# Softmax probabilities of two attention layers: halves formed in rows and transposed by DMA, in place of transposes on TensorE

## The reference, cut to what matters

```python
# layer 0
scores = jnp.einsum('bhid,bhjd->bhij', q, k) / np.sqrt(dh)
attn = jax.nn.softmax(scores, axis=-1)
out = jnp.zeros_like(q)
for r in range(Wv.shape[0]):
    v_r = (src @ Wv[r] + bv[r]).reshape(Bb, Nn, h, dh).transpose(0, 2, 1, 3)
    mask = (adj_matrix == r)[:, None]
    out = out + jnp.einsum('bhij,bhjd->bhid', attn * mask, v_r)
# ... projection, layer norm, feed forward with 1024 hidden, layer norm
# layer 1
e = jnp.einsum('whqd,whkd->whqk', q, k)
e = jnp.where(e >= 0, e, ALPHA * e)
attn = jax.nn.softmax(jnp.where(adj[:, None] > 0, e, NEG), axis=-1)
h = jnp.einsum('whqk,whkd->whqd', attn, v)
# ... layer norm, one product with the features beside it, layer norm
```

## Time and profile before

| | |
|---|---|
| median of 3 runs | 2848.8 us (2847.48 to 2848.91) |
| the profiled execution, its own time | 2849.84 us |
| its span in the trace | 2847.9 us |
| PE busy | 2697.4 us, 95% of the span |
| PE weight loads busy | 2224.1 us, 78% |
| DVE busy | 2246.5 us, 79% |
| ACT busy | 2246.4 us, 79% |
| POOL busy | 1628.7 us, 57% |
| mean granted TensorE clock | 0.988 |

### The profile page before, as it was taken

One profiled execution on the slowest core, in us unless ns is written; L12 is line 12 of the kernel. 1 busy time (PEld: TensorE's weight loads), 2 busy tenths in 40 slices (PEclk: granted clock), 3 DMA queues, 4 the chain that ended last, 5 costly groups with the idle time before them and its releaser, 6 DMA issues.

```text
span 2847.9 us, 86473 instructions
## 1 busy us (share of the span) xinstructions
PE 2697.4 (95%) x33544; PEld 2224.1 (78%) x33544; DVE 2246.5 (79%) x3986; ACT 2246.4 (79%) x6226; POOL 1628.7 (57%) x1870
## 2 busy tenths in 40 slices
PE   3899999999999999999999999999999999999985
PEld 2688888888878878878778788878788788888874
DVE  4588788888888887888888878878878878878863
ACT  3578878878878878878878878878878878878864
POOL 1355655655565565565565565565565565565563
PEclk9899999999999999999999999999999999999997
DMA  3000000000000000000000000000000000000000
GB/s 113 9 17 17 24 21 18 22 24 17 20 24 20 17 24 20 17 24 21 16 24 21 17 24 21 17 24 21 17 24 20 17 24 20 17 24 20 17 15 12
DMA packets 77909, 62.70 MB, mean 22 GB/s; under 512 B 6592, under 2 KB 76736, under 8 KB 77504
## 3 DMA queue, kind: packets, MB, share of 16 engines
q1 hardware_dynamic: 74336, 53.76, 6.2%
q10 hardware_dynamic: 3168, 3.41, 0.4%
HBM read 40.38 MB, written 16.78 MB: 20 GB/s over the span
## 4 chain that ended last, share of the span: by engine, by line
PE 55%; issue 24%; POOL 14%; DVE 4%; ACT 1%; POOLq 0%; DMA 0%; ACTq 0%
PE bank L420 40%; POOL edge_rows L1102 7%; PE bank L512 4%; PE bank L496 4%; POOL x1b L1150 3%; PE bank L484 3%; POOL oT L1169 3%; PE bank L437 3%; PE bank L465 2%; DVE o L1025 1%; DVE o_st L972 1%; DVE o_mv L976 1%; POOL o_ve L1124 0%; ACT p L705 0%; POOL o_rs L1126 0%
## 5 line engine op out<-in xcount | busy, mean ns | idle before, releaser
L935 DVE TENSOR_TENSOR pm<-pT,bank 128x4096 f16<-128x4096 f16 x256 | 568.4, 2282 | 25.8 <-issue 25.8
L420 PE MATMUL bank<-wv,xT 128*128 128x512 f16 (+1 forms) x2304 | 468.5, 344 | 0.0
L1169 POOL TENSOR_TENSOR oT<-oT_f,oT 128x512 f16<-128x512 f32 x64 | 74.4, 1163 | 606.6 <-ACT oT L805 606.6
L420 PE MATMUL bank<-yT,w 128*128 128x256 f16 x3072 | 367.1, 273 | 2.6 <-ACT oT_f L797 2.2
L705 ACT ACTIVATE p<-bank,p_nmax 128x128 f32<-128x128 f32 x1024 | 368.5, 423 | 0.0
L420 PEld LDWEIGHTS bank<-wv,xT 128*128 128x128 f16 x2304 | 226.1, 98 | 176.0 <-issue 0.3
L420 PE MATMUL bank<-w,h 128*128 128x256 f16 x3072 | 345.6, 272 | 1.7 <-POOL h L1154 1.7
L883 DVE TENSOR_TENSOR pT<-bank,pT 128x512 f16<-128x512 f32 x512 | 321.0, 675 | 10.8 <-ACT pT L779 5.8
L420 PEld LDWEIGHTS bank<-yT,w 128*128 128x128 f16 x3072 | 294.6, 98 | 40.4 <-ACT oT_f L797 2.7
L420 PEld LDWEIGHTS bank<-w,h 128*128 128x128 f16 x3072 | 295.9, 98 | 38.3 <-issue 1.9
L693 ACT ACTIVATE p<-p,p_nmax 128x128 f32<-128x128 f32 x1024 | 312.1, 390 | 0.8
(11 more groups left out here) (128 smaller groups left out, 5911.6 us busy)
## 6 DMA issues: line engine op xcount, KB each, us to landing
x_sb<-in_x_dram SPq DMA_DIRECT2D x64, 256.0 KB, 2.8
adj_i<-in_adj_dram SPq DMA_DIRECT2D x128, 128.0 KB, 2.7
out_dram<-out_sb SPq DMA_DIRECT2D x64, 256.0 KB, 2.1
pm<-in_L_gnn_W_dram ACTq DMA_DIRECT2D x1, 1024.0 KB, 14.0
pm<-in_L_gnn_W_dram SPq DMA_DIRECT2D x1, 1024.0 KB, 17.5
h_f<-in_L_gnn_Wffn_dram SPq DMA_DIRECT2D x1, 512.0 KB, 10.3
pm<-in_L_gnn_Wv_dram ACTq DMA_DIRECT2D x2, 256.0 KB, 10.6
pm<-in_L_gnn_Wv_dram SPq DMA_DIRECT2D x2, 256.0 KB, 11.0
```

What stands on the lines that cost most here:

```text
L420: last = nc.tensor.matmul(o, l, r, start=(first and k == 0), stop=(k == len(todo) - 1))
L935: V_.tensor_tensor(pm0[g][:, s], pT0[g][:, s].unsqueeze(1).broadcast_to([P, REL, HEADS, P]), edges[:, g].unsqueeze(2).broadcast_to([P, REL ...
L1169: V_.tensor_tensor(oT1[:, 1], oT1_f[:], oT1[:, 0], ALU.subtract).then_inc(S["oT1_lo"], 1)
```

## The change

In both layers the probabilities are split while they are still rows, and the halves are transposed by DMA from SBUF to SBUF:

- `transpose_probs` is gone from TensorE, and with it the eight jobs `pT0_*` and `pT1_*` of the bank table.
- Layer 0: `exp_0` writes its result back into the bank of the scores instead of `p0`; ACT copies the hi half from there into the new f16 tile `p0h` (`probs_high_0`), DVE writes the lo half (`probs_low_0`), each in four instructions by `r`. The banks of `s0_0` to `s0_3` are now freed by `p0_lo`, not by `p0_exp`.
- Layer 1: `exp_1` stays in SBUF; ACT copies the hi half into `p1h`, and POOL writes the lo half (`probs_low_1`, four instructions), which DVE did before.
- SP issues four transposing DMAs a step (`transpose_probs_0` and `transpose_probs_1`, one for each batch and layer), each of 16 blocks of 128x128 f16 with both halves of a batch: 512 KB. Before the first of a layer SP waits for all four lo halves of the pair. `by_edge_type` now waits for `pT0_in_g`, and `attend_1` for `pT1_in_g`.
- The pipeline is one pair deeper (5 instead of 4 extra steps): feed forward and the start of layer 1 now run for n-3, the attention of layer 1 for n-4, the last product for n-5. The order of jobs in all five lists is new, and so is the table of banks.
- `out_sb` is gone; the last addition is done in `x2b`, which is stored from there. Some jobs got a wait more (`values_0` for `xT0_lo`, `x_high` for q0 and k0, `x2_high` for q1 and k1).

The core of the diff (the table and the lists are cut to a few lines, since the order below shows them):

```diff
--- before.py
+++ after.py
...
 PE_BANKS = [
-    ("pT0_0", 3, 1, "pT0_lo", 4, 1),
...
+    ("v1", 1, 4, "v1_lo", 1, 1),
...
+    ("s0_0", 1, 0, "p0_lo", 4, 1),
...
-    ("s0_0", 3, 0, "p0_exp", 4, 1),
...
-        p0 = sb("p0", [ROWS, G, C, P])
+        p0h = sb("p0h", [G, 2, C, ROWS, P], F16)
+        p1h = sb("p1h", [G, 2, C, ROWS, P], F16)
...
-        pT1 = sb("pT1", [2, G, HEADS, P], F16)
+        pT1 = sb("pT1", [G, 2, HEADS, P], F16)
...
-        out_sb = sb("out_sb", [G, D])
...
+                def transpose_probs_0(m, g):
+                    sp.wait_ge(S["p0_lo"], 4 * m + 4)
+                    if past(m):
+                        sp.wait_ge(S["p0_masked"], 4 * m + 2 * g - 2)
+                    sp.dma_start_transpose(pT0[g][:].rearrange("p s h j -> p (s h) j"),
+                                           p0h[:, g].rearrange("p s c r j -> p (s c r j)")).then_inc(S[f"pT0_in_{g}"], 16)
+
+                def transpose_probs_1(m, g):
+                    sp.wait_ge(S["p1_lo"], 4 * m + 4)
+                    if past(m):
+                        sp.wait_ge(S["o1_ps"], 2 * m + g - 1)
+                    sp.dma_start_transpose(pT1[:, g].rearrange("p s h j -> p (s h) j"),
+                                           p1h[:, g].rearrange("p s c r j -> p (s c r j)")).then_inc(S[f"pT1_in_{g}"], 16)
+
                 def store(m):
                     sp.wait_ge(S["out_ready"], m + 1)
-                    sp.dma_start(out[bass.ds(m * G, G)].rearrange("g t d -> t g d"), out_sb[:]).then_inc(S["out_stored"], 16)
+                    sp.dma_start(out[bass.ds(m * G, G)].rearrange("g t d -> t g d"), x2b[:]).then_inc(S["out_stored"], 16)
 
                 def steps(n):
+                    if live(n - 1):
+                        transpose_probs_0(n - 1, 0)
                     if live(n):
                         load_x(n)
-                    if live(n - 1):
-                        load_adj0(n - 1)
+                        load_adj0(n)
+                    if live(n - 1):
+                        transpose_probs_0(n - 1, 1)
+                    if live(n - 4):
+                        transpose_probs_1(n - 4, 0)
+                        transpose_probs_1(n - 4, 1)
                     if live(n - 5):
                         store(n - 5)
-                    if live(n - 1):
-                        load_adj1(n - 1)
+                    if live(n - 2):
+                        load_adj1(n - 2)
 
                 pipeline(steps, 0, 5)
                 sp.wait_ge(S["out_stored"], 16 * PAIRS)
...
                 def values_0(m, i):
                     g, cols = i // 2, slice(i % 2 * BANK, (i % 2 + 1) * BANK)
                     bank_free(f"v0_{i}", m)
+                    pe.wait_ge(S["xT0_lo"], m + 1)
...
-                def transpose_probs(layer, p, m, g):
-                    pe.wait_ge(S[f"p{layer}_exp"], 4 * m + 4)
-                    for c in range(C):
-                        i = g * C + c
-                        bank_free(f"pT{layer}_{i}", m)
-                        for r in range(ROWS):
-                            last = nc.tensor.transpose(ps(f"pT{layer}_{i}")[:, r * P:(r + 1) * P], p[:, r, g, c], ident[:])
-                        last.then_inc(S[f"pT{layer}_ps"], 1)
-
...
-                        pe.wait_ge(S["pT1_lo"], 4 * m + 2 * g + 2)
+                        pe.wait_ge(S[f"pT1_in_{g}"], 16 * m + 16)
...
                 def steps(n):
-                    if live(n - 1):
-                        transpose_probs(0, p0, n - 1, 0)
+                    if live(n - 3):
+                        feed_forward(n - 3)
+                    if live(n - 4):
+                        values_1(n - 4)
+                    if live(n - 2):
+                        output_projection(n - 2)
...
-                        transpose_attention_1(n - 4)
+                        attend_0(n - 1, 0)
+                    if live(n - 3):
+                        scores(1, q1, k1, n - 3)
+                    if live(n - 4):
+                        attend_1(n - 4)
...
-                        act.wait_ge(S["pT1_ps"], 4 * m)
+                        act.wait_ge(S["p1_lo"], 4 * m + r - 3)
...
-                        act.wait_ge(S["pT0_ps"], 4 * m)
...
-                            last = nc.scalar.activation(p0[:, r, g, c], ps(f"s0_{r}")[:, at:at + P], ACT.Exp,
+                            last = nc.scalar.activation(ps(f"s0_{r}")[:, at:at + P], ps(f"s0_{r}")[:, at:at + P], ACT.Exp,
                                                         bias=p0_nmax[:, r, g, c:c + 1], accum_out=p0_sum[:, g, c, r:r + 1])
...
-                def probs_high_1(m, g):
-                    for c in range(C):
-                        i = g * C + c
-                        act.wait_ge(S["pT1_ps"], 4 * m + i + 1)
-                        if past(m):
-                            act.wait_ge(S["o1_ps"], 2 * m + g - 1)
-                        nc.scalar.activation(flat(pT1[:, 0, g, head_cols(c)]), ps(f"pT1_{i}")[:], copy).then_inc(S["pT1_hi"], 1)
+                def probs_high_1(m, r):
+                    act.wait_ge(S["p1_exp"], 4 * m + r + 1)
+                    if past(m):
+                        act.wait_ge(S["pT1_in_0"], 16 * m)
+                        act.wait_ge(S["pT1_in_1"], 16 * m)
+                    nc.scalar.activation(p1h[:, :, 0, :, r], p1[:, r], copy).then_inc(S["p1_hi"], 1)
...
-                def probs_high_0(m, g):
-                    for c in range(C):
-                        i = g * C + c
-                        act.wait_ge(S["pT0_ps"], 4 * m + i + 1)
-                        if past(m):
-                            act.wait_ge(S["p0_masked"], 4 * m + 2 * g - 2)
-                        nc.scalar.activation(flat(pT0[g][:, 0, head_cols(c)]), ps(f"pT0_{i}")[:], copy).then_inc(S["pT0_hi"], 1)
+                def probs_high_0(m, r):
+                    act.wait_ge(S["p0_exp"], 4 * m + r + 1)
+                    if past(m):
+                        act.wait_ge(S["pT0_in_0"], 16 * m)
+                        act.wait_ge(S["pT0_in_1"], 16 * m)
+                    nc.scalar.activation(p0h[:, :, 0, :, r], ps(f"s0_{r}")[:].rearrange("p (g c j) -> p g c j", g=G, c=C),
+                                         copy).then_inc(S["p0_hi"], 1)
...
-                def probs_low_0(m, g):
-                    for c in range(C):
-                        i = g * C + c
-                        dve.wait_ge(S["pT0_hi"], 4 * m + i + 1)
-                        low(flat(pT0[g][:, 1, head_cols(c)]), ps(f"pT0_{i}")[:], flat(pT0[g][:, 0, head_cols(c)])).then_inc(S["pT0_lo"], 1)
-
-                def probs_low_1(m, g):
-                    for c in range(C):
-                        i = g * C + c
-                        dve.wait_ge(S["pT1_hi"], 4 * m + i + 1)
-                        low(flat(pT1[:, 1, g, head_cols(c)]), ps(f"pT1_{i}")[:], flat(pT1[:, 0, g, head_cols(c)])).then_inc(S["pT1_lo"], 1)
+                def probs_low_0(m, r):
+                    dve.wait_ge(S["p0_hi"], 4 * m + r + 1)
+                    low(p0h[:, :, 1, :, r], ps(f"s0_{r}")[:].rearrange("p (g c j) -> p g c j", g=G, c=C),
+                        p0h[:, :, 0, :, r]).then_inc(S["p0_lo"], 1)
 
                 def by_edge_type(m, g):
 
-                    dve.wait_ge(S["pT0_lo"], 4 * m + 2 * g + 2)
+                    dve.wait_ge(S[f"pT0_in_{g}"], 16 * m + 16)
                     dve.wait_ge(S["edges_ps"], m + 1)
...
+                def probs_low_1(m, r):
+                    pool.wait_ge(S["p1_hi"], 4 * m + r + 1)
+                    V_.tensor_tensor(p1h[:, :, 1, :, r], p1[:, r], p1h[:, :, 0, :, r], ALU.subtract).then_inc(S["p1_lo"], 1)
...
                     pool.wait_ge(S["w_normed"], m + 1)
-                    if past(m):
-                        pool.wait_ge(S["out_stored"], 16 * m)
-                    V_.tensor_tensor(out_sb[:], w_n[:], both(g2b_row), ALU.mult).then_inc(S["out_scaled"], 1)
+                    V_.tensor_tensor(w_n[:], w_n[:], both(g2b_row), ALU.mult).then_inc(S["out_scaled"], 1)
                     pool.wait_ge(S["out_scaled"], m + 1)
                     pool.wait_ge(S["x2_plus_b"], m + 1)
-                    V_.tensor_tensor(out_sb[:], out_sb[:], x2b[:], ALU.add).then_inc(S["out_ready"], 1)
+                    V_.tensor_tensor(x2b[:], x2b[:], w_n[:], ALU.add).then_inc(S["out_ready"], 1)
```

More of the change, by code:

```diff
@@ L577, in attend_1 @@
                             last = products(ps(f"o1_{g}")[:, at:at + DH + 1],
-                                            [([pT1[:, s, g, hd] for s in range(2)], [v1[:, t, g, hd] for t in range(2)])])
+                                            [([pT1[:, g, s, hd] for s in range(2)], [v1[:, t, g, hd] for t in range(2)])])
                         last.then_inc(S["o1_ps"], 1)
@@ L655, in _ @@
-                pipeline(steps, 0, 4)
+                pipeline(steps, 0, 5)
             @block.scalar
```

399 lines of the change are left out of this document (196 added, 203 removed).

## The result

The changed kernel took **2666.1 us** in the median of 4 runs (2656.5 to 2669.0), against 2848.1 us (2847.5 to 2848.9) before: a ratio of 0.9355, with a 95% interval from 0.9337 to 0.9373. The profiled execution has a span of 2664.5 us and a mean granted clock of 0.982.

The account below looks back on a forecast made before the run. PE was taken as the bound, busy 41.72 of 42.5 us a step. 2849.8 - 222.7 + 23.7 + 39.7 = 2690.5; with the profiled execution 1.0 above the median, 2689 us, range 2640 to 2790.

Parts of the forecast that it names:

- TensorE: transposes removed: On PE, four groups of transposes at 0.87 us leave each step: 3.48 us a step, -222.7 us over 64 steps.
- C: Rival: new waits give PE back the whole 3.5 us a step and the extra step hides; 2849 us, chance 0.03.
- Deeper pipeline: A fifth partial step of filling and draining at 23.7 us: +23.7 us, bounds 0 and 39.
- New waits on PE: Four places where PE follows a chain more closely: idle 1.4 us a step against 0.78, +39.7 us.
- (d): PE's `transpose_attention_1`, 7.5 us after `attend_1`, waits for the norm's chain of about 7 us: 0 to 0.5 us.
- (b): PE's k1, one product (1.51 us) behind `transpose_x2`, waits for copy and subtraction of 1.6 us: 0.1 to 0.3 us.
- (a): PE's `values_1` waits for the lo half to free the bank of `s0_0`: idle 0.1 us, 0.3 with jitter.
- (c): PE's `hidden` behind `transpose_x1` waits for copy and subtraction: 0.2 us.
- The other engines: POOL at 30.0 us a step, ACT 36.0, DVE 35.5 at most, all under PE's 39.0: no cost.
- The transposing DMAs: SP's four transposes a step, 1.8 us each back to back and 3.9 for one alone, all hidden: 0 us.
- Rival A: DMA transposes bound: at 38 ns per 256-byte row, 4.9 us each, 2900 us or more; chance 0.18.
- The limit: Longest time per back-to-back DMA transpose before PE waits: 4.1 us, from 18.4 us for four; cover 9 us.

Follow-up runs that it names:

- plain_copy: The changed kernel with plain SBUF-to-SBUF DMA copies of the same bytes in place of the four transposing DMAs (results wrong, only time counts): 2660.4 us, ratio 0.9343.

## Why the prediction was right, and where it was off

- *TensorE: transposes removed, -222.7.* Right to the hundredth: the regular step is 42.50 - 3.48 = 39.02. The last tenth is luck: PE's busy time fell by 3.4 us a step and its idle time by 0.1. That the time comes off whole depends on the order and on where the halves are formed, though: in the old order, with all lo halves on VectorE, removing half or all of the transposes made the kernel 125 to 339 us slower. The step "it comes off whole if PE stays the bound" named the condition but put no price on it, and the one rival that stood for it, C, had the waits give back 3.5 us at the most, at 0.03; in the old order they gave back more than that. PE's busy share of 98% did not show that chains as long as PE's work ran beside it.
- *Deeper pipeline, +23.7.* 7.0 at the start and 7.0 at the end: 14.0.
- *New waits on PE, +39.7.* Mis-sized in the regular steps, where PE idles 0.7 us of 40 and not 1.4. Of the four chains (d) is the largest, 39.3 us in 60 waits for `o`, then (b), 18.2 for `xT`; (a) cost 1.9 and (c) 0.8. (a) was indeed at its limit: with four more subtractions on VectorE it cost 0.6 a step. In place of the chains came 21.6 us of long steps that I had not named, by the trace the store that holds `x2b`.
- *The other engines, 0.* POOL 30.8 (30.0 predicted), ACT 36.1 (36.0), DVE 33.6, under the 35.5 I had as the most. Only `o`'s passes grew, to 1136 ns from the 901 of the earlier trace rows; `f`'s stayed at 410.
- *The transposing DMAs, 0.* Hidden: PE waited for them three times in the whole run, and `plain_copy` is no faster. The size was off: 3.1 us of the engines each and not 1.8, 4.7 to land and not 3.9. Rival A had 38 ns a row of 256 bytes; it is 3.1 us x 16 / 2080 packets = 24 ns. The limit was off as well: with 16.9 us for four, 4.1 us each should be (16.9 - 2.1) / 4 = 3.7, and the cover was 2.1 us and not 9. Rival A, at 0.18, missed by far less than the prediction had it.
- The Trainium skill's 1309 ns for a block by DMA (VectorE: DVE Perf Modes, The three transpose paths) would have made 16 blocks an estimated 21 us. The trace doesn't agree: sixteen blocks in one DMA land in 4.7 us and take 3.1 us of the engines, 0.19 us a block.
- *Sum.* 2689 against 2666: -219 and not -223, +14 and not +24, +22 and not +40. The +22 came from another cause than the one in the sum, so that the sum came this near is in part luck. (The bounds that the prediction names add up to 2625 to 2800; it gave 2640 to 2790.)
